# Edge weights of a graph attention stage with one head: one product of 75 columns, one-hots on two engines, and score scatters two in flight

## The reference, cut to what matters

```python
def gat_layer(x, src, dst, W, a_src, a_dst, b, heads, out_ch, concat, n):
    h = (x @ W.T).reshape(n, heads, out_ch)
    alpha_src = jnp.sum(h * a_src, axis=-1)
    alpha_dst = jnp.sum(h * a_dst, axis=-1)
    e = jax.nn.leaky_relu(alpha_src[src] + alpha_dst[dst], NEG_SLOPE)
    m = jax.ops.segment_max(e, dst, num_segments=n)
    e = jnp.exp(e - m[dst])
    s = jax.ops.segment_sum(e, dst, num_segments=n)
    alpha = e / (s[dst] + 1e-16)
    return jax.ops.segment_sum(alpha[:, :, None] * h[src], dst, num_segments=n)
```

## Time and profile before

| | |
|---|---|
| three runs | 10313.65, 10321.53, 10325.05 us |
| median | 10321.53 us |
| the profiled execution, its own time | 10293.34 us |
| its span, first to last instruction | 10291.6 us |
| granted TensorE clock, mean | 0.764 |
| PE, DVE, ACT, POOL busy | 6457.9, 5072.5, 2679.0, 3711.5 us |
| loops of the two H = 1 stages | from 3523 to 3678 us and from 6191 to 6346 us of the span |
| loops of the three H = 4 stages | from about 2566, 5307 and 7551 us on |

### The profile page before, as it was taken

How to read it: one execution, slowest core, us unless ns; L and a number is a source line. 1 busy time by engine, 2 the same in 40 slices (tenths; PEclk the granted TensorE clock), 3 DMA queues, 4 the chain that set the end, 5 groups by cost and what they waited for, 6 DMA issues and landing times. The chain is left out here.

```text
span 10291.6 us, 89481 instructions
## 1 busy us (share of the span) xinstructions
PE 6457.9 (63%) x25974; PEld 4026.9 (39%) x25974; DVE 5072.5 (49%) x10547; ACT 2679.0 (26%) x6047; POOL 3711.5 (36%) x3723
## 2 busy tenths in 40 slices
PE   6847455797477545469964553654853677537756
PEld 6723233343455323247743232332442333213334
DVE  7831465222777543621056554446563888543121
ACT  0122000222444123112224431321232555212211
POOL 2626465001366256220044744650121555110111
PEclk5579666899699766679977765666876899768868
DMA  4200233101366233114433324330030222210012
GB/s 108 62 6 10 78 92 78 38 28 39 112 178 179 74 108 90 43 56 164 149 84 94 91 66 127 92 78 2 15 105 28 68 68 67 69 46 8 7 62 78
DMA packets 440685, 758.49 MB, mean 74 GB/s; under 512 B 172573, under 2 KB 268795, under 8 KB 437521
## 3 DMA queue, kind: packets, MB, share of 16 engines
q0 software_dynamic: 182080, 437.26, 15.7%
q1 hardware_dynamic: 239987, 295.32, 9.1%
q10 hardware_dynamic: 18136, 20.19, 0.6%
HBM read 669.59 MB, written 82.56 MB: 73 GB/s over the span
## 5 line engine op out<-in xcount | busy, mean ns | idle before, releaser
L2456 POOL DMA_INDIRECT R<-table,edges x1248 | 1242.0, 995 | 813.8 <-issue 292.9
L2508 DVE TENSOR_TENSOR acc<-acc,PS 125x256 f32 (+3 forms) x1664 | 704.7, 423 | 1206.5 <-PE PS L2525 506.1
L2525 PE MATMUL PS<-R,hot 128*125 128x256 f32 (+1 forms) x1664 | 690.7, 555 | 490.3 <-issue 313.4
L2525 PEld LDWEIGHTS PS<-R,hot 128*125 128x125 f32 x1664 | 383.4, 261 | 797.5 <-issue 635.9
L2468 ACT ACTIVATE R<-R,TW 128x128 f32<-128x128 f32 (+1 forms) x1248 | 494.0, 431 | 672.9 <-DMA R<-table,edges 631.3
L2276 PE MATMUL PS<-S,hotT 125*128 125x100 bf16 (+1 forms) x6240 | 364.1, 219 | 474.7 <-DVE hotT L2383 399.7
L2523 PE MATMUL PS<-R,hot 128*125 128x258 f32 x1664 | 446.3, 420 | 193.1 <-DVE acc L2506 116.3
L2456 POOL DMA_INDIRECT xx<-table,edges x416 | 414.9, 997 | 380.9 <-PE PS L2525 308.1
L2456 POOL DMA_INDIRECT room<-table,edges x416 | 427.8, 1028 | 297.2 <-PE PS L2525 124.5
L2276 PEld LDWEIGHTS PS<-S,hotT 125*128 125x128 bf16 x6240 | 316.4, 113 | 523.1 <-DVE hotT L2383 364.8
L1759 POOL DMA_INDIRECT sorted_edges<-edge_rows,edge_place x391 | 399.5, 1022 | 321.7 <-DVE edge_place L1997 113.5
(11 more groups left out here) (718 smaller groups left out, 13360.8 us busy)
## 6 DMA issues: line engine op xcount, KB each, us to landing
rowb<-slo_row SPq DMA_DIRECT2D x260, 250.0 KB
W<-in_L_ffn_W1p SPq DMA_DIRECT2D x32, 1024.0 KB
W<-in_L_ffn_W2p SPq DMA_DIRECT2D x32, 1024.0 KB
near<-dst_row SPq DMA_DIRECT2D x98, 256.0 KB
R<-table,edges POOLq DMA_INDIRECT x1248
W<-in_L_ffn_w SPq DMA_DIRECT2D x16, 1024.0 KB
hib<-hi_mask SPq DMA_DIRECT2D x260, 50.0 KB
g<-gate_rows POOLq DMA_DIRECT2D x8, 1568.0 KB
```

The source lines that it names most:

```text
L2456: pool.indirect_dma_start(self.R[:, u, 0:self.W], None, self.table[:, :], bass.IndirectOffsetOnAxis(ap=self.G.edges[:, g, 0:1], axis=0)).t ...
L2508: v.tensor_tensor(to, to, self.G.PS[0:P, self.bank + k, 0:self.WH], ALU.add).then_inc(self.put, 1)
L2525: mm = pe.matmul(self.G.PS[0:P, self.bank + k, 0:self.WH], hot, self.R[:, u, :], start=True, stop=True)
```

## The change

With H = 1 only: RR is 3 instead of 4; the three parts lie side by side in one product of 75 columns (4 products a quad instead of 12); `prod` holds 4 x 75 instead of 4 x 25 columns, and `total` sums over 75; odd one-hots are made on ACT by the code that served H = 4, and a row load waits for both kinds of one-hots. With every H: a scatter of POOL waits until the one two before it has landed, with a semaphore for the even and one for the odd ones.

```diff
--- before.py
+++ after.py
@@ -2185,7 +2185,7 @@
 
 
 
-    TH, RR, NQ = T * H, 4, ET // 4
+    TH, RR, NQ = T * H, 3 if H == 1 else 4, ET // 4
     fill = G.fills[H]
     lag = 14
     with Stage(nc) as s:
@@ -2193,7 +2193,8 @@
         rowb = [s.sb(f"rowb{j}", [P, 1024], BF16) for j in range(RR)]
         hib = [s.sb(f"hib{j}", [128, 8, T], BF16) for j in range(RR)]
         hotT = [s.sb(f"hotT{j}", [P, 512], BF16) for j in range(3)]
-        prod = [s.sb(f"prod{j}", [128, 4, H, T]) for j in range(2)]
+        parts = 3 if H == 1 else 1
+        prod = [s.sb(f"prod{j}", [128, 4, parts * H, T]) for j in range(2)]
         S1 = s.sb("S1", [128, ET, H])
         dT = s.sb("dT", [TT, CT, 128, H]) if spare is None else spare[0:TT, CT:2 * CT, :].unsqueeze(3)
         d0 = s.sb("d0", [TT, CT, H])
@@ -2203,10 +2204,10 @@
         sc = s.sb("sc", [TT, 2, CT, H])
         one, top, wide = s.sb("one", [TT, 1]), s.sb("top", [1, 1]), s.sb("wide", [TT, 1])
         got, got_hi = [[s.sem(f"{x}{j}") for j in range(RR)] for x in ("got", "got_hi")]
-        far, apart = s.sb("far", [P, 512], BF16) if H > 1 else None, s.sem("apart")
-        hot_odd = s.sem("hot_odd")
-        split, hot, gathered, taken, summed, steps, dmoved, dgot, dload, zturned, tail, ready, rows_done, exp_done, back, out = [
-            s.sem(x) for x in ("split", "hot", "gathered", "taken", "summed", "steps", "dmoved", "dgot", "dload", "zturned", "tail",
+        far, apart = s.sb("far", [P, 512], BF16), s.sem("apart")
+        hot_odd, dmoved = s.sem("hot_odd"), [s.sem(f"dmoved{j}") for j in range(2)]
+        split, hot, gathered, taken, summed, steps, dgot, dload, zturned, tail, ready, rows_done, exp_done, back, out = [
+            s.sem(x) for x in ("split", "hot", "gathered", "taken", "summed", "steps", "dgot", "dload", "zturned", "tail",
                                "ready", "rows", "exp", "back", "out")]
         PS = G.PS
         ready_at = [-(-(g + 1) * TT // 4) for g in range(CT)]
@@ -2218,9 +2219,12 @@
             @block.gpsimd
             def _(pool):
                 for t in range(T):
+                    if t >= 2:
+                        pool.wait_ge(dmoved[t % 2], 16 * (t // 2))
                     pool.indirect_dma_start(fill[:, :], bass.IndirectOffsetOnAxis(ap=G.first_at[:, t:t + 1], axis=0),
-                                            AL[:, t, H:2 * H], None).then_inc(dmoved, 16)
-                pool.wait_ge(dmoved, 16 * T)
+                                            AL[:, t, H:2 * H], None).then_inc(dmoved[t % 2], 16)
+                for j in range(2):
+                    pool.wait_ge(dmoved[j], 16 * len(range(j, T, 2)))
                 for g in range(CT):
                     pool.indirect_dma_start(d0[:, g, :], None, fill[:, :],
                                             bass.IndirectOffsetOnAxis(ap=G.tile_first[:, g:g + 1], axis=0)).then_inc(dgot, 16)
@@ -2237,9 +2241,8 @@
             def _(sp):
                 def rows(k):
                     if k >= RR:
-                        sp.wait_ge(hot, (k - RR + 1) * (1 if H > 1 else 2))
-                        if H > 1:
-                            sp.wait_ge(hot_odd, k - RR + 1)
+                        sp.wait_ge(hot, k - RR + 1)
+                        sp.wait_ge(hot_odd, k - RR + 1)
                     sp.dma_start(rowb[k % RR][:, :], over(G.slo_row[k * 1024:(k + 1) * 1024], P)).then_inc(got[k % RR], 16)
 
                 def masks(k):
@@ -2265,13 +2268,14 @@
                     mm.then_inc(zturned, 1)
 
                 for n in range(NQ):
-                    if H == 1:
-                        pe.wait_ge(hot, n + 1)
-                    else:
-                        pe.wait_ge(hot_odd if n % 2 else hot, n // 2 + 1)
+                    pe.wait_ge(hot_odd if n % 2 else hot, n // 2 + 1)
                     if n >= 4:
                         pe.wait_ge(taken, n - 3)
                     for f in range(4):
+                        if H == 1:
+                            mm = pe.matmul(PS[:, n % 4, f * 3 * T:(f + 1) * 3 * T], hotT[n % 3][:, ts(f, 128)],
+                                           S3[:, :, :, :].rearrange("p j h t -> p (j h t)"), start=True, stop=True)
+                            continue
                         for j in range(3):
                             mm = pe.matmul(PS[:, n % 4, f * TH:(f + 1) * TH], hotT[n % 3][:, ts(f, 128)],
                                            S3[:, j, :, :].rearrange("p h t -> p (h t)"), start=(j == 0), stop=(j == 2))
@@ -2312,7 +2316,7 @@
 
             @block.scalar
             def _(act):
-                for n in range(1, NQ, 2) if H > 1 else []:
+                for n in range(1, NQ, 2):
                     act.wait_ge(got[(n // 2) % RR], 16 * (n // 2 // RR + 1))
                     if n >= 3:
                         act.wait_ge(hot_odd, n // 2)
@@ -2345,13 +2349,14 @@
                     v.wait_ge(got_hi[(n // 2) % RR], 16 * (n // 2 // RR + 1))
                     if n >= 2:
                         v.wait_ge(summed, n - 1)
-                    v.tensor_tensor(prod[n % 2][:, :, :, :], PS[:, n % 4, 0:4 * TH].rearrange("p (f h b) -> p f h b", f=4, h=H),
-                                    hib[(n // 2) % RR][:, 4 * (n % 2):4 * (n % 2) + 4, :].unsqueeze(2).to_broadcast([128, 4, H, T]),
+                    v.tensor_tensor(prod[n % 2][:, :, :, :], PS[:, n % 4, 0:4 * parts * TH].rearrange("p (f h b) -> p f h b", f=4, h=parts * H),
+                                    hib[(n // 2) % RR][:, 4 * (n % 2):4 * (n % 2) + 4, :].unsqueeze(2).to_broadcast([128, 4, parts * H, T]),
                                     ALU.mult).then_inc(taken, 1)
 
                 def total(n):
                     v.wait_ge(taken, n + 1)
-                    v.tensor_reduce(S1[:, 4 * n:4 * n + 4, :], prod[n % 2][:, :, :, :],
+                    p = prod[n % 2][:, :, :, :]
+                    v.tensor_reduce(S1[:, 4 * n:4 * n + 4, :], p.rearrange("p f (h j) b -> p f h (j b)", h=H),
                                     AX.X, ALU.add).then_inc(summed, 1)
 
                 def chunk(g):
@@ -2376,7 +2381,7 @@
                     c(ins)
 
                 for n in range(NQ + 1):
-                    if n < NQ and (H == 1 or n % 2 == 0):
+                    if n < NQ and n % 2 == 0:
                         if n >= 3:
                             v.wait_ge(gathered, n - 2)
                         v.wait_ge(got[(n // 2) % RR], 16 * (n // 2 // RR + 1))
```

## The result

| | before | after |
|---|---|---|
| median | 10309.7 us (12 runs, 10290.9 to 10325.1) | 10339.4 us (12 runs, 10319.7 to 10367.5) |
| span of the profiled execution | 10291.6 us | 10365.9 us |
| ratio, 95% interval | | 1.0034, 1.0025 to 1.0044 |

The change makes the kernel slower by 0.34%, some 30 us: inside the range, 9 us over the forecast of 10330, and just beyond what I had set as "no change" (21 us).

What follows compares the result with a forecast made beforehand. Bound by POOL's issuing during scatters and by a ring of mask and row loads in the one-head gather phases. Four-head stages -12, one-head +10 and +11 make +9 on the 10321.5 us median: 10330 us, range 10288 to 10356.

Steps and rivals of the forecast that it cites:

- The two phases: All five stages: takes are slow while POOL issues scatters (2.21 us a quad in the first), faster behind them (1.32).
- Step 1: One-head stages: 4 products instead of 12 and odd one-hots on ACT gain nothing in the gather phase; take some 460 ns.
- Step 2: One-head gather phase: two pairs in the ring of loads instead of three; a pair costs 3.15 us against 2.66.
- Step 3: All stages: with two scatters in flight, each landing in 3.8 us, 25 take 47.5 us; a quad costs 1.65 us.
- rival B: Besides A, gaps between scatters give PE all it needs: 1.28 us a quad, -12 per four-head stage, 10283 us; chance 10%.
- d0, dT and the gathers of all stages come 10 us later: All stages: 25 scatters take 47.5 us instead of 37, so the loads POOL issues behind them start 10 us later.
- Four-head stages: Stages one, three and five: -4 us each, together -12, from 1.65 us a quad during scatters.
- Second stage: First one-head stage: loop +7.5 us after cover, POOL's last gather +10; the later decides, +10.
- Fourth stage: Second one-head stage: 40 gathers, POOL ends 13 us sooner, so the loop decides: +11 us.
- A: One-head stages: with fewer DMAs the mask lands in 4 us beside gathers, a pair costs 2.55, 10306 us; chance 15%.
- C: One-head stages: two pairs are too few; a mask needs 5.9 us, a pair 3.5, +29 in all, 10350 us; chance 20%.
- D: Scatters never wait, landing within 2.96 us; PE gains nothing, one-head stages lose +8 and +11, 10340 us; chance 5%.

Runs made afterwards that it cites:

- rr3: The kernel before with only RR = 3 in the one-head stages; 10295.4 us against 10260.3 for before, ratio 1.0036.
- free: The changed kernel with its scatters issued without a wait, as before; 10275.6 us against 10260.3 for before, ratio 1.0014.
- late: The changed kernel with its first chunk at quad 60 instead of 40; 10259.5 us against 10260.3 for before, ratio 0.9998.
- two_late: The kernel before with scatters at most two in flight and the first chunk at quad 60; 9909.4 us against 9873.2 for before, ratio 1.0036.
- both: late with four mask buffers and the mask loads issued one pair earlier; 9915.0 us against 9873.2 for before, ratio 1.0043.
- two: The kernel before with only its scatters limited to two in flight; 10314.5 us against 10260.3 for before, ratio 1.0054.
- ref: The kernel before timed against itself and profiled again; 10302.0 us against 10298.9, ratio 1.0002.
- third: The changed kernel unaltered, run and profiled again on a third chip; 10346.8 us against 10298.9 for before, ratio 1.0047.
- best: Four-head stages as in late, one-head stages as in mixed; 10255.3 us against 10298.9 for before, ratio 0.9954.
- mixed: both, with the scatter limit and late first chunk only in the four-head stages; 9888.7 us against 9873.2 for before, ratio 1.0015.
- unmerged: best without merge, with RR = 4 and one-head one-hots on DVE; 10228.7 us against 10262.8 for before, ratio 0.9966.

## Why the prediction was right or wrong

**The two phases.** Right: the slow quads belonged to POOL's issuing. With POOL at 44% instead of 76% PE's results no longer hold up a four-head stage (1.15 us a quad).

**The number.** It lies in the range, and that is in part luck. The four-head stages were to give 12 us back and took 15 more. By the stages the change costs 44 us in its first profile, not 9; on the 10321.5 us that I started from, this would be 10365, past the upper end of 10356. The median of before came down to 10309.7 with twelve runs, and the time outside of the stages was 14 us shorter for the changed kernel.

**Step 1, merge worth nothing.** The take was right (0.46 forecast, 0.45 to 0.47 measured). The price was not: 20 to 23 us, the difference of `rr3` and `free`, though 18 of it in one stage. I had counted the shorter way from take to next mask issue (1.1 us) under the ring without saying that the merge pays for it. The sum is not touched by this.

**Step 2, RR = 3.** Mechanism and size right: mask issue to take 4.83 and 5.02 (5.2 forecast), take to issue 1.07 (1.1), a pair 2.92 and 3.00 (3.15).

**Step 3, scatters.** Two terms wrong and one consequence missed. A scatter takes 5.2 us to land, not 3.8: 3.8 was read from the end, where no further scatter follows. So 25 scatters are 61 to 66 us, not 47.5. A quad costs 1.15 us, not 1.65; the gaps are all that PE needs, which is rival B's condition and more. And **"d0, dT and the gathers of all stages come 10 us later"** is the step that failed: I followed the gathers to who waits for them, but not dT. Its reader stands at quad 40. At 1.65 us a quad and 47.5 us of scatters it would have been reached behind dT's landing; at 1.15 and 61 to 66 it is reached 14 to 22 us ahead of it. The two errors make 92 us of wait together. Each alone would have made 2 to 3 us a stage, by an estimate from the first stage, where the first take lies 9.2 us behind the first scatter and dT 13.3 behind the last: quad 40 at 54 us and dT at 57 with fast quads only, 72 and 74 with slow scatters only.

**The sum.** Four-head stages: -4 forecast, +3.0, +5.1 and +7.1 measured: a gain of 14 to 16 and a wait of 19 to 22. Second stage +10 forecast for POOL's last gather, +10.6 measured, and its issue does end 10.5 us later (169.7 to 180.2 us from the meeting). But two errors cancel in it: the first gather came 28 us later, not 10, and 48 gathers then took 105 us instead of 122. The loop, with DVE's stand of 16 us in it, arrives at the same time. So the match is luck. Fourth stage +11 forecast, +18.0 (21 and 13 in the other two profiles), with a stand of 14 us in it. Together +9 forecast, +44 in the profile (+47, +35), +30 in the runs. Two slips of arithmetic move the forecast by under 2 us: 3580 + 105.5 + 2 is 3687.5, not 3688.5, and a last gather at 3704 is 11.5 us behind 3692.5, not 10.

**The rivals.** A's landing of 4 us did not come (4.8 to 5.0). The landing did fall with fewer loads in flight, from 6.4 to 4.9 us. That agrees in direction with the Trainium skill's "DMA: Bandwidth & Descriptors" (latency and other measured facts), by which the fixed cost of a transfer shrinks with a lighter load on HBM. No run tells such a lighter load from a shorter queue of loads; beside the gathers the core moved 151 GB/s, after 161 before. B was right for the four-head stages, hidden by a wait; `late` shows its -12. C did not come in its own way, though its total (+29) did. D is refuted: POOL waited at 82 of 125 scatters.

## What to carry to other kernels

When a stream is slowed on purpose to free an engine, follow each of its products to its first reader, and compare when that reader arrives *at the new pace*: here the freed engine ran into the throttled one. Keep an order of work (a lag, a chunk's place) and a throttle together; moving one number from 40 to 60 turned a loss of 44 us in these stages into a gain of 26 (in the runs, into no difference from before). And price a smaller ring with what shortens its other leg: the two were in one change, and each hid a part of the other. Where two engines end a stage, compare the time of each, not the stage's length: in `two_late` and `both` a loop 12 to 14 us shorter did not show. And time a cure for waits on more than one chip: on the second one all four variants tried were slower than before.

## What the runs showed of the hardware

**Work of PE becomes visible late while POOL issues indirect DMAs back to back, on some chips.** In the touched stages `late` and `free` show it, and `two` most plainly, as it changes nothing else. Its one-head quads during the scatters, with the same 12 products, the same DVE work and the same granted clock of 0.50, take 1.2 us where they took 2.1 to 2.2 (means from the fifth take to the last), so it is not the clock. The same delay is seen in 26 of the 30 us ahead of them. At about 540 us, in code that the change doesn't touch, PE makes 56 small products (L1733) while POOL issues scatters (L1759) back to back, and DVE waits for them to copy the result (L1740). The line's page, before and after:

```profile
L1733 PE MATMUL PS<-A,Wt x56: 352/361/361, 504.2 to 515.9; 128*128 128x8 f32 x32, 128*128 128x2 f32 x24
```

```profile
L1740 DVE COPY O<-PS x5: 150/163/175, 542.3 to 542.6; 128x16 f32<-128x16 f32 x3, 128x8 f32<-128x8 f32 x1, 128x4 f32<-128x4 f32 x1
```

```profile
L1733 PE MATMUL PS<-A,Wt x56: 164/353/378, 508.4 to 542.0; 128*128 128x8 f32 x32, 128*128 128x2 f32 x24
its engine sat idle before it (us, times) until:
  issue: 42.8, 32
```

```profile
586.92 0.96 POOL L1759 DMA_INDIRECT sorted_edges<-edge_rows,edge_place  x1 [0.30 <-issue]
...
595.36 0.48 DVE L1740 COPY O<-PS 128x16 f32<-128x16 f32 x5 [81.78 <-remote]
```

Before, the last product began at 515.9 and DVE's copy at 542.3, 26 us later. In the changed kernel's profile the same products trickle until 542.0 with nothing to wait for in the program, and the copy begins at 595.4, 53 us later and 8 us behind POOL's last scatter. The DMA engines are at 2 to 4% there, so it is not their load. In the profiles on chips of the same pace this place ends 6 to 36 us later than in before's first one (8 in `ref`, 6 in `third`, 36 in `best`), without relation to the change. Which part of the chip holds PE's signals back, the trace does not name.

**The second chip does not show it.** In `again`, the changed kernel on that chip, POOL issues the same scatters back to back through this place (one each 1.26 us), and the copy begins 0.05 us behind the modelled end of the last product:

```profile
498.30 12.09 PE L1733 MATMUL PS<-A,Wt 128*128 128x8 f32 x56
```

```profile
510.44 0.48 DVE L1740 COPY O<-PS 128x16 f32<-128x16 f32 x5 [9.33 <-PE PS L1733]
```

It is so in all four profiles of that chip (0.4 us from the start of the last product), where in nine of the ten profiles of the other chips it follows after 18 to 78 us (in `best` the products themselves come so late, at 593 us, that the scatters are over, the last at 586). And that chip is faster where POOL issues most: of the 382 us between the profiles of `after` and `again`, 353 lie in five of the six stages in which POOL issues 368 to 416 gathers (L2461), 63 to 81 in each. *Busy time* in the stage behind the first `edge_weights`, `after` and then `again`, each with a line of *the page of L2511*, DVE's wait for PE there (us, times):

```profile
2795.00:3437.00 642.00, 451.99 (x1664) 315.08 (x1664) 467.43 (x729) 287.65 (x832) 429.67 (x416) 0.91 0.61 171
```

```profile
  PE PS L2528: 72.8, 56
```

```profile
2705.00:3267.00 562.00, 417.72 (x1664) 289.58 (x1664) 468.50 (x728) 287.62 (x832) 415.95 (x416) 0.97 0.69 195
```

```profile
  PE PS L2528: 6.7, 13
```

Over all fourteen profiles this wait for PE is 4 to 7 us on the second chip and 60 to 78 on the others. The stage is 80 us shorter there, and 66 of them are in this wait; that all of the 353 us are of this kind was not shown.

**What stays open.** Among the variants of one chip the differences of the medians follow those of the stage sums within 13 us (`two` less `free`: 39 and 34; `again` less `mixed`: 86 and 90; `third` less `best`: 91 and 86). Before alone does not fit: against them its time outside of the stages (median less stage sum, with 919.5 us for its stages where it has no profile) is shorter by 12 to 25 us on the first of these chips, by 54 to 58 on the second, by 7 to 13 on the third, by 14 beside `unmerged`, and 14 us longer where the change was first timed. For the smaller differences the place at 540 us is a candidate; that it is the cause was not shown.

For the second chip the 919.5 us are the doubtful number, as before has no profile there. If PE's results do not come late on it, the scatters slowed nothing down in the kernel before, and its stages were shorter. With the time outside of the stages that the four variants share (9007 to 9011 us), the 9873.2 us of before leave 862 to 866 us for them, an estimate. The changed kernel's 967 us are then 101 to 105 over before, and the runs show 101. So on that chip the limit on scatters probably had nothing to give and kept its whole cost. A profile of before on that chip would settle it; none was taken. The change costs 35 to 47 us by its stages on the chips where before was profiled, and 30, 48 or 101 by the runs.
